# Four row maxima turned by one product, and a newly planned list of entries, in an attention and expert kernel

## What is computed

```python
x = L0_attn_input_data                          # (2, 2048, 128)
xn = layernorm(x)
scores = einsum('bsd,de,bte->bst', xn, qk, xn) / sqrt(128)      # causal
attn = einsum('bst,btd,de->bse', softmax(scores), xn, ov)
# one of E = 8 experts per row, by the largest product with a centroid
eid = argmax(xn @ centroids.T); alpha = sigmoid(xn . centroids[eid])
ffn = relu((layernorm(xn) * ln_g[eid] + ln_b[eid]) @ w1[eid] + b1[eid]) @ w2[eid] + b2[eid]
out = x + attn + xn + alpha * ffn
```

## Time and profile before

| | |
|---|---|
| median of three timed executions | 223.56 us |
| lowest and highest of them | 223.23 and 226.32 us |
| span of the profiled execution, first to last instruction | 223.1 us |
| PE, DVE, ACT, POOL busy | 92%, 79%, 70%, 69% of the span |
| granted PE clock, mean of the span | 0.985 of full |

### The profile page before, as it was taken

The page is one execution under the profiler, slowest core; times in us unless marked ns, Lnnn a source line. Parts: engine busy times, 40 slices in busy tenths (PEclk is TensorE's granted clock), DMA queues, the critical chain, the costliest instruction groups (busy, mean ns, idle before and its releaser), DMA issues.

```text
span 223.1 us, 6878 instructions
## 1 busy us (share of the span) xinstructions
PE 206.3 (92%) x2428; PEld 159.9 (72%) x2428; DVE 175.5 (79%) x448; ACT 155.2 (70%) x346; POOL 154.3 (69%) x230
## 2 busy tenths in 40 slices
...
GB/s 167 314 289 64 6 0 94 116 355 232 5 12 39 36 39 39 44 43 40 36 40 36 128 198 160 125 92 141 131 150 92 50 40 37 38 35 172 256 193 141
DMA packets 37601, 23.55 MB, mean 106 GB/s; under 512 B 12472, under 2 KB 34144, under 8 KB 37568
## 3 DMA queue, kind: packets, MB, share of 16 engines
q1 hardware_dynamic: 34960, 18.28, 32.3%
...
## 4 chain that ended last, share of the span: by engine, by line
PE 77%; DVE 11%; ACT 4%; issue 4%; DMA 2%; SPq 1%; DVEq 0%; ACTq 0%
PE psum L1343 6%; PE psum L1300 6%; PE psum L1301 6%; PE psum L1302 6%; PE psum L1351 6%; PE psum L1344 6%; PE psum L1277 5%; PE psum L1460 4%; PE psum L1461 4%; PE psum L1462 4%; PE psum L1434 4%; PE psum L1436 4%; PE psum L1435 4%; PE psum L1260 3%; PE psum L1334 2%
## 5 line engine op out<-in xcount | busy, mean ns | idle before, releaser
L910 DVE TENSOR_TENSOR p_lo<-p_sb,p_hi 128x512 f16<-128x512 f32 (+1 forms) x68 | 42.0, 638 | 12.2 <-ACT p_sb L1050 12.0
L1044 ACT ACTIVATE p_hi<-psum 128x512 f16<-128x512 f32 (+1 forms) x68 | 37.1, 547 | 19.4 <-PE psum L1351 14.2
L1050 ACT ACTIVATE p_sb<-psum 128x512 f32<-128x512 f32 (+1 forms) x80 | 42.5, 539 | 6.8 <-PE psum L1334 6.7
L693 POOL DMA_INDIRECT sorted_y<-xn x39 | 38.1, 977 | 11.6 <-ACT xn L1174 5.5
L1018 DVE SCALAR_TENSOR_TENSOR h_lo<-psum,h_hi 128x512 f16<-128x512 f32 x39 | 26.8, 690 | 21.5 <-ACT h_hi L1166 18.7
L671 POOL MEMSET v_full<- 1x600 f32 x71 | 41.7, 588 | 0.0
L684 POOL DMA_INDIRECT sorted_x<-xr,pos x32 | 33.5, 1047 | 11.9 <-issue 11.4
L1166 ACT ACTIVATE h_hi<-psum 128x512 f16<-128x512 f32 x39 | 23.3, 597 | 21.0 <-PE psum L1436 19.2
L1343 PE MATMUL psum<-v_hi,p_hi 128*128 128x129 f16 x236 | 32.7, 220 | 1.2 <-DVE x_sb L927 1.2
L896 DVE TENSOR_REDUCE row_max<-psum 128x1 f32<-128x512 f32 x48 | 32.3, 682 | 1.6 <-PE psum L1277 1.1
L1344 PE MATMUL psum<-v_lo,p_hi 128*128 128x128 f16 x236 | 32.6, 219 | 0.0
...
## 6 DMA issues: line engine op xcount, KB each, us to landing
...
sorted_y<-xn POOLq DMA_INDIRECT x39
sorted_x<-xr,pos POOLq DMA_INDIRECT x32
```

The costliest lines, as they stand in the source:

```text
L693: pool.indirect_dma_start(out=sorted_y[:, :], out_offset=bass.IndirectOffsetOnAxis(ap=tokens, axis=0), in_=xs[:, t % SLOTS, 0:P], in_offse ...
L910: v.tensor_tensor(p_lo[:, u, off:GW], p_sb[:, u, off:GW], p_hi[:, u, off:GW], ALU.subtract).then_inc(s_plo, 1)
L1044: a.activation(p_hi[:, u, off:GW], bank[SCORE[n % R]][:, off:GW], ACT.Exp, scale=SCALE).then_inc(s_exph, 1)
L1050: a.activation(p_sb[:, u, off:GW], bank[SCORE[n % R]][:, off:GW], ACT.Exp, scale=SCALE).then_inc(s_exp, 1)
```

## The change

A group's four maxima now stand 32 columns apart in one stationary matrix of 128 columns, one product turns them, and SHa copies four rows of 128 that lie 32 partitions apart. Beside it the whole list is written anew: the same 1120 entries in another order, on every engine. No other line changes.

```diff
-        max_col = sb("max_col", [P, GT, P], F16)
+        max_col = sb("max_col", [P, GT, P // GT], F16)
...
-                    a.activation(qT_hi[0:1, k * GW:(k + 1) * GW], bank[bank_of["SH", b, g]][0:1, :], ACT.Copy,
-                                 bias=SHIFT, scale=1.0 / W_SCALE).then_inc(s_shift, 1)
+                    for i in range(GT):
+                        turned = bank[bank_of["SH", b, g]][i * (P // GT):i * (P // GT) + 1, 0:P]
+                        ins = a.activation(qT_hi[0:1, k * GW + i * P:k * GW + (i + 1) * P], turned, ACT.Copy,
+                                           bias=SHIFT, scale=1.0 / W_SCALE)
+                    ins.then_inc(s_shift, 1)
...
-                for i in range(GT):
-                    m = mm(at[:, i * P:(i + 1) * P], max_col[:, i, :], minus16[:], start=True, stop=True)
-                m.then_inc(s_negT, 1)
+                mm(at[:, 0:P], flat(max_col[:]), minus16[:], start=True, stop=True).then_inc(s_negT, 1)
```

The list, read for one engine at a time, in the stretches that the prediction speaks of (- before, + after):

```diff
 ACT, start
-BIASa LE.0.1 C0a AE.0 AE.1 AE.2 C1a LE.1.2 C2a Ta.0 W1h.0 W1h.1 Ta.1 W1l.0 Qa.0 Vf.0 LE.2.3
+LE.0.1 BIASa C0a C1a LE.1.2 C2a AE.0 Ta.0 AE.1 AE.2 AE.3 W1h.0 Ta.1 LE.2.3 AE.4 LE.3.4 Qa.0
 DVE, start
-VAR.0.1 VAR.1.2 BIAS RN.0.1 ROW.0.1 C2v C1v Tl.0 ROW.1.2 VAR.2.3 VAR.3.4 Tl.1 Ql.0 VAR.4.6 MR.0.0.0.0 Ql.1
+VAR.0.1 VAR.1.2 RN.0.1 ROW.0.1 BIAS C2v C1v Tl.0 ROW.1.2 VAR.2.3 VAR.3.4 Tl.1 VAR.4.6 Ql.0 Ql.1 MR.0.0.1.0
 PE, start
-WU C0 C1 C2 T.0 W1.0 W1.1 T.1 W1b.0 Q.0 V.0 W1.2 W1b.1 M.0.0.0.0 Q.1 M.0.0.3.0 W1.3
+WU C0 C1 C2 T.0 W1.0 T.1 W1b.0 V.0 Q.0 Q.1 W1.1 W1.2 M.0.0.1.0 W1b.1 M.0.0.0.0 M.0.0.2.0 M.0.0.3.0
 POOL, up to SC.0
-RN.1.2 MISC BASE.0 BASE.1 RN.2.3 Vl.0 RN.3.4 BASE.2 RN.4.6 BASE.3 RN.6.8 W2l.0 W2l.1 BASE.4 BASE.5 BASE.6 BASE.7 W2l.2 W2l.3 COL0 S.0
+RN.1.2 MISC BASE.0 BASE.1 RN.2.3 RN.3.4 RN.4.6 W2l.0 RN.6.8 Vl.0 BASE.2 W2l.1 BASE.3 BASE.4 BASE.5 BASE.6 COL0 S.0 S.1 W2l.2
 SP, whole
-W1.0 W1.1 W2l.0 W2l.1 W2l.2 Z.0 W2l.3 W1.2 Z.1 Z.2 W2l.4 W1.3 Z.3
+W1.0 W1.1 W1.2 W1.3 W2l.0 W2l.1 Z.0 Z.1 W2l.2 Z.2 Z.3 W2l.3 W2l.4
 DVE, choice of experts
-RM.0.2 MR.0.3.1.0 MR.0.3.3.1 MR.0.3.2.0 MR.0.3.1.1 CH.0 MR.0.3.0.3 CH.1 Sl.0 SIG PL MR.0.3.3.2 Vl.2 QT.0.1.0 QT.0.1.1
+RM.0.2 Ql.3 MR.0.3.3.1 CH.0 CH.1 SIG MR.0.3.2.0 PL Sl.0 QT.0.1.0 MR.0.3.1.3 MR.0.3.0.1 MR.0.3.1.1 QT.0.1.1
 DVE, last rows to send
-XL.30 MR.1.1.2.1 XL.31 XL.32 RM.1.1 MR.1.2.3.1 Sl.6 Sl.7 MR.1.2.2.1 XL.33 XL.34
+XL.32 MR.1.1.2.1 MR.1.1.0.0 XL.33 MR.1.1.0.1 Sl.6 RM.1.1 XL.34
+QT.0.3.0 QT.0.3.1 XL.40 XL.41 Sl.7 W1l.6 XL.42
 PE and DVE, into the expert stage
-PE  P.50 PB.49 P.51 HI.0 PB.50 PB.51 HI.1 HI.2 OUT.0 OUT.1 HI.3
+PE  P.50 PB.49 PB.50 P.51 M.1.3.0.2 PB.51 HI.0 M.1.3.0.0 M.1.3.0.1 HI.1 HI.2 OUT.0 HI.3
-DVE RM.1.2 W1l.7 Ql.7 MR.1.3.0.1 XL.47 XL.48 XL.49 XL.50 XL.51 QT.1.1.0 QT.1.1.1 LO.0
+DVE XL.50 Ql.7 XL.51 QT.1.1.0 RM.1.2 QT.1.1.1 LO.0
```

More of the change, by code:

```diff
@@ L68 @@
 ORDER = entries("""
[L69 to L83, removed]
@@ L94 @@
[L94 to L98, removed]
@@ L109 @@
[L109 to L123, removed]
@@ L129 @@
-X.79 P.75 PB.75 P.76 PB.76 P.77 EH.77 EX.77 EH.78 EX.78 PB.77 P.78 P.79 PB.78 EH.79 EX.79 QT.1.3.0 QT.1.3.1 SO.38 PB.79
+VAR.0.1 WU LE.0.1 C0 BIASa VAR.1.2 C0a RN.0.1 C1 C1a ROW.0.1 LE.1.2 C2a C2 BIAS C2v AE.0 Ta.0 T.0 AE.1 W1.0 C1v Tl.0
+RN.1.2 MISC ROW.1.2 AE.2 T.1 AE.3 BASE.0 VAR.2.3 VAR.3.4 BASE.1 W1b.0 W1h.0 Tl.1 RN.2.3 Ta.1 LE.2.3 V.0 AE.4 Q.0 Q.1
+VAR.4.6 W1.1 Ql.0 W1.2 Ql.1 M.0.0.1.0 MR.0.0.1.0 LE.3.4 W1b.1 Qa.0 M.0.0.0.0 W1l.0 M.0.0.2.0 M.0.0.3.0 RN.3.4
+MR.0.0.0.0 MR.0.0.2.0 Qa.1 V.1 RN.4.6 MR.0.0.3.0 W1b.2 VAR.6.8 T.2 Vf.0 W1h.1 XA.2 AE.5 W1.3 W2l.0 W1h.2 W1l.1 RM.0.0
```

82 lines of the change are left out of this document (57 added, 25 removed).

## The result

The kernel after takes 222.79 us (median of 20 runs, 220.97 to 225.30) beside 224.25 us of the kernel before in the same series. The ratio is 0.9933, with a 95% interval of 0.991 to 0.9957. So it is faster by 0.7%, some 1.5 us; the forecast was 219.5 us, 1.8% less. Ratios leave out runs of over 1.5% above the kernel's fastest, here seven of 224.29 us and more with a mean clock of 0.976 to 0.984; the medians of all 20 runs give 0.9935. The runs differ by whole falls of TensorE's granted clock: twelve have a mean clock of 0.991 or 0.992 and took 222.1 to 223.1 us, the one with 1.000 took 220.97 us, and by the same steps those seven have two or three falls.

A forecast was written before the change was run, and what follows sets the result against it. DVE sets the pace first, then DVE and PE are both full, then PE alone. Start 1.3, idle 1.2 and 0.8, one MR 0.6 give 3.9, plus 0.1: 4.0 off the 223.56 median, 219.5 us; range 216.3 to 224.0.

The forecast's parts named there:

- I put the change on the median: Whole-kernel sum: the 4.0 us change was taken from the median of the runs shown, 223.56, giving 219.5 us.
- The start: Start-up to Tl.0: U_sb comes earlier by 1.3 us, so Tl.0 moves from 12.17 to 10.9 us; -1.3 us.
- slow clock prolonged: Rival, before DVE's first MR: W1.1 and W1.2 run at half clock, +1.7 us, 221.2 us in all; chance 0.13.
- DVE up to the expert stage: Two stages before the expert stage: DVE idles less, -1.2 and -0.8 us; one MR moves behind LO.0, -0.6.
- The index and SC.0: Ahead of the sends: the index comes at 58.5 us and SC.0 moves from 63.67 to 60.1 us.
- The work is the same, so only idle time can go: DVE before the expert stage: unchanged work, idle 3.9 and 2.6 us, of which some 1.5 us of links stay.
- Before, SC.28 stood at 114.1 us and HI.0 came 12.1 us later: Sends to expert stage: the 12.1 us distance was kept, so SC.28 at 110.5 puts HI.0 at 122.6 us.
- OUT.0 has no wait for LO.0: Entry to the expert stage: OUT.0 comes at 125.15 us by HI.0 and by LO.0 alike, -3.9 us.
- Sl.7 and SC.28 met: Late sends: SC.28 at 110.5 us needs Sl.7, now expected at 110.4, so the two meet.
- The turn: Eight groups: PE gains 1.4 us by 24 fewer products; ACT's 1.8 us more is costed at nothing.
- I take 0.8 us: ACT's four row copies per group: 0.8 us, between 0.58 and 1.1; 0.2 us more per group than before.
- The sum: Span: 223.1 - 3.9 - 0.1 = 219.1 us; behind HI.0 one M more is +0.2, two SH -0.3.

The follow-up runs named there:

- e14: The kernel before, unchanged, profiled again: span 221.4 us with a mean clock of 1.000.
- e4: The kernel after with 14 extra products filling PE's wait for the one-hot sums ahead of the counts: 222.45 us, ratio 0.9928 to the kernel before.
- e11: The kernel after with extra products filling PE's waits at the counts (14) and for p_lo at PB.48 (10): 220.90 us, ratio 0.9894 to the kernel before.
- e10: The kernel before, old list, with the new turn and 16 extra products filling PE's start wait for U_sb: 223.54 us, ratio 1.0016 to the kernel before.
- e12: The kernel after with the old turn, its waits at the counts and for p_lo filled with extra products: 222.55 us, ratio 0.9972 to the kernel before.

## Why the prediction was wrong

**The base.** "The span is 0.1 us below the lowest and 0.5 below the median of the runs shown; I put the change on the median." This step failed first. The profiled execution was one of the longer ones: its device time was some 224.9 us, and its forecast span of 219.1 means 220.85 us, not 219.5. So 1.35 us of the missed 3.3 are the base: 0.7 the median of three runs (223.56 us; 224.25 of 20), the rest the long execution. The start was read from it too. Tl.0 moved from 12.17 to 9.82 us, 2.35 us for the 1.3 forecast, but in e14 it stands at 10.69 in the unchanged list, so the change won 0.9 us there; the W1 pair at full clock e14 has as well.

**The clock.** The rival "slow clock prolonged" had the mechanism and the wrong place. W1.1 and W1.2 ran at full clock (1.02 us); the fall came behind the counts and cost 1.57 us (e4) to 1.8 us (e11, by X.12). Of 222.79 - 220.85 = 1.94 us that is nearly all. The Trainium skill (TensorE: Matmul & The Clock Gate, HAM oscillation — how this bites in real kernels) says of a wait that returns with each tile of a loop that it makes PE start slow again each time; here one wait of 3.15 us does it once, and the wait for `U_sb` at the start did it in one execution of the kernel before (1.98 us) and not in e14 (1.96).

**DVE up to the expert stage.** The index and SC.0 came better than forecast (58.99 us for 60.1), and DVE's idle time in the first stage fell by 1.7 us instead of 1.2; in the second it grew by 0.3 us instead of falling by 0.8. Two steps failed. "The work is the same, so only idle time can go": DVE was busy for 2.7 us longer in the two stages, as its steps beside POOL took longer. And "Before, SC.28 stood at 114.1 us and HI.0 came 12.1 us later" (by the trace 114.31 and 11.9): SC.28 came at 110.9 us and HI.0 14.2 us later. I followed DVE and the sends and took PE to come along; its idle time was to fall with DVE's, and it grew from 1.7 to 3.0 us in the second stage and from 6.4 to 8.2 in the first. No step of mine asked what PE has left to do while DVE chooses the experts, nor what POOL does beside DVE: the trace of before has the same stretched low parts (three L910 in 3.25 us at 121.85 us, beside W2l.5 and W2l.6, where the two of 118.35 us take 1.29), only hidden.

**What held.** With the clock kept up, the forecast is close: e11 has HI.0 at 122.88 us (122.6 forecast), a span of 219.0 us (219.1) and 220.9 us (220.85 on the right base). Part of that is luck: SC.28 comes at 109.65 us, 0.85 ahead of the forecast, and HI.0 13.2 us behind it instead of 12.1. In the kernel after OUT.0 has no wait for LO.0, Sl.7 and SC.28 met without a loss, and PE is full behind.

**The turn.** "I take 0.8 us" for four copies: it is 1.06 us, near the upper bound, 0.5 us more than before per group, and with the clock kept up no run shows that it costs time (e10: +0.26 us, inside its interval). The sum gave the turn 0.3 us behind HI.0; behind HI.0 it is 0.5 between e12 and e11. The 1.65 us that it is worth under the new list, for nothing under the old, hold the low part that is hit, which no term of mine had.
